# Self attention of a decoder layer: rotated q and k split in high and low parts, far scores as three rounded products

## What is computed

```python
q = einsum('bpd,hde->bphe', x, W_Q) + b_Q     # the same for k and v
q, k = rotary(q), rotary(k)
scores = where(causal, einsum('bqhd,bkhd->bhqk', q, k) / sqrt(128), 0)
max_v = max(abs(scores)); sgn = sign(scores)
attn_w = sgn * exp(sgn * scores - max_v)
attn = attn_w / (sum(abs(attn_w)) + 1e-6)
out = einsum(einsum(v, attn), W_O) + b_O
```

## Time and profile before

| | us |
|---|---|
| median of three runs | 1519.03 |
| lowest and highest | 1518.56, 1520.51 |
| the profiled execution | 1520.14 |
| its span, first to last instruction | 1517.1 |
| TensorE busy | 1397.2 (92%) |
| VectorE busy | 1219.8 (80%) |
| ScalarE busy | 802.9 (53%) |
| GpSimd busy | 668.4 (44%) |

### The profile page before, as it was taken

How to read it: one execution, slowest core, us unless ns; L and a number is a source line. 1 busy time by engine, 2 the same in 40 slices (tenths; PEclk the granted TensorE clock), 3 DMA queues, 4 the chain that set the end, 5 groups by cost and what they waited for, 6 DMA issues and landing times.

```text
span 1517.1 us, 25412 instructions
## 1 busy us (share of the span) xinstructions
PE 1397.2 (92%) x8594; PEld 1097.6 (72%) x8594; DVE 1219.8 (80%) x1990; ACT 802.9 (53%) x1798; POOL 668.4 (44%) x749
## 2 busy tenths in 40 slices
PE   5899999999999999999999999889999998359886
PEld 4788888888888888888888888776777776213332
DVE  6988888888888888888887888636788887669996
ACT  4444444445444443455465465445555555258884
POOL 4434335234334334443433432352345553448984
PEclk9999999999999999999999999989999999779998
DMA  5401101011010110021112010240000004014433
GB/s 209 157 11 42 46 25 42 28 43 42 28 43 23 38 52 15 15 70 57 36 42 91 28 63 29 70 126 15 15 15 15 14 0 172 3 30 92 91 85 93
DMA packets 73380, 79.93 MB, mean 53 GB/s; under 512 B 46006, under 2 KB 46518, under 8 KB 72892
## 3 DMA queue, kind: packets, MB, share of 16 engines
q1 hardware_dynamic: 73276, 78.73, 17.0%
HBM read 59.83 MB, written 8.40 MB: 45 GB/s over the span
## 4 chain that ended last, share of the span: by engine, by line
PE 50%; DVE 29%; issue 10%; POOL 7%; ACT 2%; DMA 1%; DVEq 1%; SPq 0%; POOLq 0%; ACTq 0%
PE psum L326 9%; PE psum L328 8%; PE psum L327 8%; DVE rope_b L513 6%; PE psum L939 4%; PE psum L940 3%; PE psum L941 3%; PE psum L367 3%; DVE p L522 3%; DVE total_e L526 3%; DVE acc L556 3%; DVE s L494 2%; PE psum L1007 2%; PE psum L388 2%; DVE rope_a L513 2%
## 5 line engine op out<-in xcount | busy, mean ns | idle before, releaser
L730 POOL TENSOR_TENSOR qk<-rope_a,rope_b 128x512 f32<-128x512 f32 x128 | 177.4, 1386 | 569.3 <-DVE rope_b L513 569.3
L326 PE MATMUL psum<-x_hi,w_hi 128*128 128x512 f32 x512 | 210.8, 412 | 11.4 <-POOL w_lo L724 11.4
L328 PE MATMUL psum<-x_hi,w_lo 128*128 128x512 f32 x512 | 201.7, 394 | 0.0
L327 PE MATMUL psum<-x_lo,w_hi 128*128 128x512 f32 x512 | 200.8, 392 | 0.0
L513 DVE SCALAR_TENSOR_TENSOR rope_b<-psum,qk_bias,sin 64x512 f32<-64x512 f32 x256 | 192.0, 750 | 3.7
L604 ACT ACTIVATE e<-s 128x384 f32<-128x384 f32 x128 | 66.4, 519 | 242.6 <-DVE s L494 242.6
L494 DVE SCALAR_TENSOR_TENSOR s<-psum,tri 128x384 f32<-128x384 f32 x128 | 70.8, 553 | 121.2 <-PE psum L367 121.2
L326 PE MATMUL psum<-w_hi,x_hi 128*128 128x256 f32 x512 | 147.4, 288 | 0.0
L327 PE MATMUL psum<-w_lo,x_hi 128*128 128x256 f32 x512 | 144.7, 283 | 0.0
L328 PE MATMUL psum<-w_hi,x_lo 128*128 128x256 f32 x512 | 144.6, 282 | 0.0
L618 ACT ACTIVATE e<-p 128x128 f32<-128x128 f32 x128 | 39.5, 309 | 184.2 <-DVE p L522 184.2
(11 more groups left out here) (183 smaller groups left out, 3796.3 us busy)
## 6 DMA issues: line engine op xcount, KB each, us to landing
stage<-w_self_dram SPq DMA_DIRECT2D x64, 256.0 KB, 2.9
w_raw<-w_ffn_dram SPq DMA_DIRECT2D x32, 512.0 KB, 3.6
acc<-xT_dram SPq DMA_DIRECT2D x4, 1024.0 KB, 7.6
acc<-x_dram SPq DMA_DIRECT2D x1, 4096.0 KB, 14.7
w_signs<-w_sign SPq DMA_DIRECT2D x16, 256.0 KB, 2.1
c_raw<-ctxT_dram SPq DMA_DIRECT2D x8, 512.0 KB, 3.6
xstage<-w_cross_dram SPq DMA_DIRECT2D x16, 256.0 KB, 3.0
w<-w_signs SPq DMA_DIRECT2D x2, 2048.0 KB, 12.1
```

What stands on the lines that cost most here:

```text
L326: pe.matmul(ps, ah, bh, start=n == 0, stop=False)
L327: pe.matmul(ps, ah, bl, start=False, stop=False)
L328: last = pe.matmul(ps, al, bh, start=False, stop=n == len(pairs) - 1)
L730: nc.gpsimd.tensor_tensor(qk[:, k % 2, which, :], rope_a[:, which, :], rope_b[:, which, :], ALU.add).then_inc(qk_ready, 1)
```

## The change

After the rope, q and k are split like the other operands. GpSimd sums `rope_a` and `rope_b` in place into `rope_a` (`add_rope`), ScalarE rounds the sum to `qk_hi` (`round_qk`), GpSimd subtracts to `qk_lo` (`split_qk`). The near product takes the float32 sum straight from `rope_a`; the far product becomes `three` on the split operands. `qk`, which held two units, is gone; the new tiles hold one, and so `rope` and `round_qk` wait until the scores of the unit before are done.

The written orders change too. On TensorE the query projection comes first in the slot, ahead of the scores, `turn` 1 moves behind the key projection, and output 0 of even slots moves ahead of `mix`. On VectorE `mask_and_max` moves behind `z_low`, `v_out` and the addition of the even slot's second output. On ScalarE `round_qk` for q stands before `totals`, for k at the slot's end. On GpSimd the sum and subtraction of q, then those of k, stand before `norm`.

```diff
@@ score
-                q, kk = qk[:, k % 2, 0, :], qk[:, k % 2, 1, :]
-                pe.matmul(psS[b][:, 0:P], q[:, b * S:b * S + P], kk[:, b * S:b * S + P],
-                          start=True, stop=True)
-                pe.matmul(psS[b][:, P:LW], q[:, b * S + P:(b + 1) * S], kk[:, b * S:(b + 1) * S],
-                          start=True, stop=True).then_inc(scores, 1)
+                near, far = slice(b * S, b * S + P), slice(b * S + P, (b + 1) * S)
+                pe.matmul(psS[b][:, 0:P], rope_a[:, 0, near], rope_a[:, 1, near], start=True, stop=True)
+                both = slice(b * S, (b + 1) * S)
+                three(psS[b][:, P:LW], [(qk_hi[:, 0, far], qk_lo[:, 0, far], qk_hi[:, 1, both], qk_lo[:, 1, both])]
+                      ).then_inc(scores, 1)
@@ tensor: emit
+                if live(t, 0):
+                    project(t, k, 0)
                 if live(t, 1):
                     score(t - 1, k - 1, 0)
                     score(t - 1, k - 1, 1)
...
                 if live(t, 2):
                     turn(t - 2, 0)
-                if live(t, 0):
-                    project(t, k, 0)
-                if live(t, 2):
-                    turn(t - 2, 1)
                 if odd and o_live(t, k):
                     output(t, k, 0)
                 if live(t, 0):
                     project(t, k, 1)
-                if odd and o_live(t, k):
-                    output(t, k, 1)
+                if live(t, 2):
+                    turn(t - 2, 1)
+                if o_live(t, k):
+                    output(t, k, 1 if odd else 0)
                 if live(t, 2):
                     mix(t - 2, (k - 2) % 8, 0)
                     mix(t - 2, (k - 2) % 8, 1)
-                if not odd and o_live(t, k):
-                    output(t, k, 0)
@@ rope
                 wait(dve, qk_ready, (t - 1) * 2 + which + 1)
+                wait(dve, scores, (t - 1) * 2 + 2)
@@ vector: emit
-                if live(t, 1):
-                    mask_and_max(t - 1, 0)
-                    mask_and_max(t - 1, 1)
                 if live(t, 3):
                     z_low(t - 3, (k - 3) % 8)
                 if live(t, 1):
                     v_out(t - 1, (k - 1) % 8, v_bias[:, bass.ds(group(t, k, i, 1) * 256, 256)])
                 if odd and live(t, 5):
                     add_output(t - 1, (k - 1) % 8, 1)
+                if live(t, 1):
+                    mask_and_max(t - 1, 0)
+                    mask_and_max(t - 1, 1)
@@ scalar
+            def round_qk(t, which):
+                act.wait_ge(qk_summed, t * 2 + which + 1)
+                wait(act, scores, (t - 1) * 2 + 2)
+                nc.scalar.copy(qk_hi[:, which, :], rope_a[:, which, :]).then_inc(qk_rounded, 1)
...
                     take_turned(t - 2, 1)
+                if live(t, 0):
+                    round_qk(t, 0)
                 if live(t, 1):
                     totals(t - 1, 0)
                     totals(t - 1, 1)
...
                 ffn_pieces(t, k, i)
+                if live(t, 0):
+                    round_qk(t, 1)
@@ gpsimd
+            def add_rope(t, which):
                 pool.wait_ge(qk_turned, t * 2 + which + 1)
-                wait(pool, scores, (t - 2) * 2 + 2)
-                nc.gpsimd.tensor_tensor(qk[:, k % 2, which, :], rope_a[:, which, :], rope_b[:, which, :],
-                                        ALU.add).then_inc(qk_ready, 1)
+                nc.gpsimd.tensor_tensor(rope_a[:, which, :], rope_a[:, which, :], rope_b[:, which, :],
+                                        ALU.add).then_inc(qk_summed, 1)
+
+            def split_qk(t, which):
+                pool.wait_ge(qk_rounded, t * 2 + which + 1)
+                nc.gpsimd.tensor_tensor(qk_lo[:, which, :], rope_a[:, which, :], qk_hi[:, which, :].bitcast(F32),
+                                        ALU.subtract).then_inc(qk_ready, 1)
...
-                elif live(t, 0):
-                    add_rope(t, k, 0)
-                    add_rope(t, k, 1)
+                if live(t, 0):
+                    add_rope(t, 0)
+                    split_qk(t, 0)
...
+                if live(t, 0):
+                    add_rope(t, 1)
+                    split_qk(t, 1)
```

More of the change, by code:

```diff
@@ L152, in self_attention @@
         z_lo = sb("z_lo", [P, 2, 2, W], F32R)
-        qk = sb("qk", [P, 2, 2, W])
+        qk_hi = sb("qk_hi", [P, 2, W], F32R)
+        qk_lo = sb("qk_lo", [P, 2, W], F32R)
         rope_a = sb("rope_a", [P, 2, W])
@@ L178, in self_attention @@
         qk_turned = sem("qk_turned")
+        qk_summed = sem("qk_summed")
+        qk_rounded = sem("qk_rounded")
         qk_ready = sem("qk_ready")
@@ L725, in split_low @@
                                         ALU.subtract).then_inc(w_ready, 1)
-            def add_rope(t, k, which):
+            def add_rope(t, which):
                 pool.wait_ge(qk_turned, t * 2 + which + 1)
-                wait(pool, scores, (t - 2) * 2 + 2)
-                nc.gpsimd.tensor_tensor(qk[:, k % 2, which, :], rope_a[:, which, :], rope_b[:, which, :],
-                                        ALU.add).then_inc(qk_ready, 1)
+                nc.gpsimd.tensor_tensor(rope_a[:, which, :], rope_a[:, which, :], rope_b[:, which, :],
[4 more added lines that the diff above has]
+                                        ALU.subtract).then_inc(qk_ready, 1)
             def norm(u, b):
@@ L757, in emit @@
                     split_low(Q1, 0)
-                    add_rope(t, k, 0)
+                if live(t, 0):
+                    add_rope(t, 0)
+                    split_qk(t, 0)
+                if isinstance(t, int) and t == 0:
                     split_low(K1, 0)
-                    add_rope(t, k, 1)
+                if live(t, 0):
+                    add_rope(t, 1)
+                    split_qk(t, 1)
+                if isinstance(t, int) and t == 0:
                     split_low(O0, 0)
                     split_low(O1, 0)
-                elif live(t, 0):
-                    add_rope(t, k, 0)
-                    add_rope(t, k, 1)
                 if live(t, 1):
```

## The result

The changed kernel takes 1545.95 us (median of 4, 1545.63 to 1548.61) where the kernel before takes 1518.80 in the same comparison: a ratio of 1.0181, 95% interval 1.0163 to 1.0199. That is +27 us where +36 was forecast, inside the range and on the side forecast.

The account below looks back on a forecast made before the run. TensorE and VectorE were taken as nearly balanced, bound by the loop score, VectorE, second output, next score. Pairs +26.7, groups' first slots +3.7, start +4 and end +1.5 gave +36, 1555 us; range 1525 to 1580.

Parts of the forecast that it names:

- The loop through add_output: Score, VectorE's chain, second output, next score: the query projection enters this path, even slots +1.17 us, odd ones -0.28.
- The pair: One even and one odd slot together: +0.89 us, over thirty undisturbed pairs +26.7 us.
- the walk: Step-by-step timing of an even slot from its first score product, 14.97 us before, 16.14 after; chance of this case 0.75.
- The products: Far score as three rounded products instead of one float32: 0.075 us saved a score, vanishing in even slots' wait.
- The split at nothing: Two more casts on ScalarE and two more subtractions on GpSimd per slot, costed at nothing; cover 1.2 us in odd slots.
- GpSimd against VectorE: GpSimd's sums keep holding times_sign and total_e, 2.03 and 1.49 us stand; the new q subtraction adds nothing.
- the rule that the prediction cites: Two-SBUF-input VectorE instructions and SBUF-reading GpSimd instructions block each other entirely, the first to start wins.
- Rival A: VectorE's chain at least 1.9 us shorter than walked, even slots' wait gone, products' saving shows: -9.6, 1509 us; chance 0.08.
- The first slot of a group: z_low and v_out, now ahead of the mask, wait for z_high behind four weight casts: +0.5 us, seven times, +3.7.
- The start: Second slot's query projection waits for x_lo pieces until 28.63, first scores at 31.4 instead of 24.78: +4 us (0 to 7).
- The end: No query projection covers the last split: +1.5 us (0 to 3).

Follow-up runs that it names:

- far_float32: The changed kernel with the far product as one float32 product, split still made and waited for: 1553.47 us against 1519.31 (1.0227).
- add_early: The changed kernel with add_output 0 of even slots moved behind times_sign, ahead of both inversions, on VectorE: 1497.79 us against 1519.31 (0.9864).
- order_only: The kernel before with only the new written orders of TensorE and VectorE, float32 scores and no split: 1549.67 us against 1519.31 (1.0193).
- tiny_split: The changed kernel with the split's casts and subtractions handling 2 columns of 512 from the second unit on: 1540.09 us against 1517.93 (1.0137).
- split_only: The changed kernel with the old orders of TensorE and VectorE put back, split and rounded products kept: 1539.45 us against 1519.31 (1.0131).
- tiny_sum: The changed kernel with GpSimd's sums handling 2 columns of 512 from the second unit on: 1480.94 us against 1518.80 (0.9751).
- z_high_first: The changed kernel with z_high ahead of the weight casts on ScalarE: 1540.87 us against 1517.93 (1.0140).
- no_waits: The changed kernel with add_output 0 earlier in even and odd slots and z_high ahead of the weight casts: 1489.49 us against 1517.93 (0.9813).

## Why the prediction was right, point by point

The terms can be counted in the trace, from first score products. The kernel before, then the changed one:

```profile
145.11 0.27 PE L365 MATMUL psum<-qk 128*128 128x128 f32 x1
...
862.70 0.27 PE L365 MATMUL psum<-qk 128*128 128x128 f32 x1
...
966.63 0.27 PE L365 MATMUL psum<-qk 128*128 128x128 f32 x1
```

```profile
29.43 0.58 PE L368 MATMUL psum<-rope_a 128*128 128x128 f32 x1 [4.13 <-POOL qk_lo L745]
...
72.99 0.38 PE L368 MATMUL psum<-rope_a 128*128 128x128 f32 x1 [0.99 <-POOL qk_lo L745]
...
152.61 0.27 PE L368 MATMUL psum<-rope_a 128*128 128x128 f32 x1
...
889.97 0.27 PE L368 MATMUL psum<-rope_a 128*128 128x128 f32 x1
...
994.72 0.38 PE L368 MATMUL psum<-rope_a 128*128 128x128 f32 x1 [1.25 <-POOL qk_lo L745]
```

Units 8 to 56, 48 slots: 737.36 against 717.59 us, +19.8. Up to unit 8 it is +7.5, of which 2.76 is only that the scores now stand behind P0, and 1.6 the clock in one slot. Where the self attention ends shows in the last but one unit's scores and in the first transpose of the cross attention, before and then after:

```profile
951.86 0.27 PE L365 MATMUL psum<-qk 128*128 128x128 f32 x1
...
1006.67 0.27 PE L980 MATMUL psum<-ident,x 128*128 128x128 f32 x1
```

```profile
981.59 0.27 PE L368 MATMUL psum<-rope_a 128*128 128x128 f32 x1
...
1032.77 0.27 PE L998 MATMUL psum<-ident,x 128*128 128x128 f32 x1
```

At the transpose the changed kernel is 26.1 us behind: 0.15 by the fourth unit's scores (P0's 2.76 taken off), 26.8 in the 59 slots after them, -0.9 at the end. The forecast for these three was 4, 30.4 and 1.5. The spans differ by 29.7, but the runs do not put the other 3.6 down to the change. The feed forward part is the same in both kernels, and one stretch of it, up to the first product of its second layer, took 34.1 us at a granted clock of 0.71 against 29.7 us at 0.84 before; in `far_float32`, again with the same code there, it took 29.6. So the trace says +26 and the medians +27.

*The loop through add_output.* Right in place and kind, and nearly in size. Even slots +1.10 (forecast +1.17), odd ones -0.29 (-0.28); removed by `add_early`, present in full in `order_only`. The pair was mis-sized by 0.08, 2.4 us over 30 pairs, from small roundings in each link of the walk. A little more is that slots 5, 6 and 0 of a group were longer than the two that I took as common, before the change more than after it (14.92, 15.18 and 15.10 against 14.58, 16.16 and 16.6), and that one slot before took 16.19: some 3 us.

*The products.* Right: 0.08 a score, hidden in the waits and shown by `far_float32`.

*The split at nothing.* Right in common slots, by `tiny_split`, and the q subtraction and the k part came within 0.3 us of the walk (7.7 to 9.0, and 13.24 for 13.5). With the new orders put back as a whole (`split_only`), P0 among them, the split costs 22 us; that P0 is the cover is the prediction's reading, and the waits for the split fit it.

*GpSimd against VectorE.* Right as it stood, 2.10 and 1.07 us unchanged. One reading there is loose: the rule that the prediction cites is worded for VectorE instructions with two inputs in SBUF, as `times_sign` has, while `total_e` reads only `total`. Its 1.08 against 0.17 us shows that a GpSimd sum holds it too, and `tiny_sum` confirms that, but it is no test of the rule as worded. Rival A named this as what would have to go, and `tiny_sum` is that case: 38 us faster than before instead of the 9.6 in the rival's price, since with the waits gone slots drop to TensorE's own time, and the 0.55 and 0.35 us that the kernel before waits go as well, which the rival's price left out.

*The first slot of a group.* +0.5 forecast, 16.62 against 16.11 in `z_high_first`: right.

*The start.* The failed term, in size and in mechanism: +4 us forecast, next to nothing measured. The prediction let P0 of the second slot wait for the `x_lo` pieces, done at 28.63. In the changed kernel it did not wait; its first and last product were

```profile
22.39 0.40 PE L329 MATMUL psum<-x_hi,w_hi 128*128 128x512 f32 x1
...
24.91 0.39 PE L331 MATMUL psum<-x_hi,w_lo 128*128 128x512 f32 x1
```

while VectorE still made those pieces, until 27.93:

```profile
22.18 5.75 DVE L456 TENSOR_TENSOR x_lo<-acc,x_hi 128x512 fp32r<-128x512 f32 x4
```

They belong to the next pair of batches: `project` waits for `x_split` only where the head is the first of its group, and the second slot projects the second head of the same pair. The first score did come late (29.43, forecast 31.4), but for another reason, the k split, 4.13 us in the row above. The two halves of the change show it apart, `order_only` first, then `split_only`:

```profile
24.91 0.38 PE L365 MATMUL psum<-qk 128*128 128x128 f32 x1 [0.46 <-POOL qk L728]
```

```profile
29.44 0.58 PE L368 MATMUL psum<-rope_a 128*128 128x128 f32 x1 [7.99 <-POOL qk_lo L747]
```

The order alone leaves the first score where it was (24.78); the split moves it. That the number for the first score was near was luck. The delay is then lost again: the fourth unit's scores came at 70.08 before, waiting 1.97 us for GpSimd:

```profile
70.08 0.38 PE L365 MATMUL psum<-qk 128*128 128x128 f32 x1 [1.97 <-POOL qk L730]
```

After, they come at 72.99. Less the 2.76 that P0 takes ahead of them, that is +0.15. Before the scores of units 1 to 3 TensorE used to wait for GpSimd for 3.04, 0.81 and 1.97 us, now, behind P0, for 2.33, 0.94 and 0.99, though GpSimd has the split to do as well. In `split_only`, with the old orders, the waits for the split are 5.01, 3.33 and 2.77, and the slots 16.6 to 17.6 instead of 14.3 to 14.7.

*The end.* +1.5 forecast, -0.9 measured. The term that was named is right: the last score waits 1.25 us for the split, and `tiny_split` shows 1.4. But between the last score and the first transpose of the cross attention the changed kernel takes 2.0 us less (38.05 against 40.04), and the prediction had nothing for that; `order_only` has it too (37.4), so it comes with the order.

The start (3.9), the end (2.4), the pairs (2.4) and the unequal slots (some 3), less the 1.6 that the clock added in one slot, are the 10 us between 36 and the 26 of the trace. What made the prediction right is its account of the common slots, which hold most of the time.

## What to carry to other kernels

Where two engines are nearly balanced, walk one turn of the loop between them and ask of each moved step whether it enters or leaves that loop; a step that only changes places can cost more than all new instructions. An addition that frees a single buffer should stand as early in its engine's order as its data allow. Before a costlier arithmetic is taken to save time on the busiest engine, remove the waits of that engine: here two moved additions gave 28 us, and the three rounded products 7 at most.

## What the runs showed of the hardware

The granted clock fell after one of the long waits for the addition and not after the others. In the changed kernel TensorE idled 2.10 us before 146.82, and its next products are spaced 0.43 us where they are spaced 0.23 elsewhere (window: length, busy of the engines, granted clock, DMA):

```profile
146.82 0.79 PE L329 MATMUL psum<-w_hi,z_hi 128*128 128x512 f32 x1 [2.10 <-DVE acc L558]
147.41 0.63 PE L330 MATMUL psum<-w_lo,z_hi 128*128 128x512 f32 x1
147.84 0.63 PE L331 MATMUL psum<-w_hi,z_lo 128*128 128x512 f32 x1
```

```profile
147.00:150.00 3.00, 3.00 (x8) 2.32 (x9) 1.51 (x3) 0.07 (x1) 2.80 (x5) 0.50 0.00 0
```

A granted clock of 0.50 is the lower level, 1.2 GHz. It lengthened that slot from 16.6 to 18.2 us. The waits in the same place of five later groups were 2.09 or 2.10 us too and left the clock as it was. In `order_only` and in `far_float32` these waits are shorter, 1.96 to 1.98 us, and the clock fell after three of the six in each. So the length of the wait alone does not tell when it falls; what does was not tried.

The second thing is idle time on VectorE of up to 3.78 us for which the profile names nothing, at a slot in which a turn of the loops begins, in `no_waits`:

```profile
778.13 0.69 DVE L548 TENSOR_TENSOR z_lo<-psum,z_hi 128x512 fp32r<-128x512 f32 x1 [3.78 <-issue]
```

It occurs four times between 100 and 960 us. `add_early` has it four times too (2.9 to 3.5 us), and its slots there take 15.9 to 16.5 us. In the kernels with slack on VectorE it is hidden but for single slots; what it is was not tried.
